# A fused attention block whose matrix work is all put into 64x32 tiles, in one order per step

## The reference, cut to what matters

```python
x = x + attn(layernorm(x))
x = x + ffn(layernorm(x))          # ternary weights, 4-bit and 8-bit activations, inner size 1376

q, k, v = proj(w_q), proj(w_k), proj(w_v)        # (2, 32, 1024, 16)
scores = einsum('bhqd,bhkd->bhqk', q, k) / sqrt(16)
out = einsum('bhqk,bhkd->bhqd', softmax(scores), v)
attn = einsum('bse,oe->bso', out, w_o)
```

## Time and profile before

| | |
|---|---|
| time, median of 3 runs (lowest to highest) | 963.26 us (963.06 to 964.16) |
| profiled execution: its time, its span | 963.78 us, 962.0 us |
| mean granted clock of TensorE | 0.987 |
| busy share of the span: PE, PEld, DVE, ACT, POOL | 93%, 31%, 88%, 78%, 24% |
| the same from 200 to 700 us | 96%, 27%, 95%, 87%, 31% |
| score, transposed score, projection piece, values: mean duration of one matmul | 384, 385, 377, 606 ns |
| DVE maximum, ACT exponential: mean duration of one | 683, 606 ns |

### The profile page before, as it was taken

One profiled execution on the slowest core, in us unless ns is written; L12 is line 12 of the kernel. 1 busy time (PEld: TensorE's weight loads), 2 busy tenths in 40 slices (PEclk: granted clock), 3 DMA queues, 4 the chain that ended last, 5 costly groups with the idle time before them and its releaser, 6 DMA issues.

```text
span 962.0 us, 17694 instructions
## 1 busy us (share of the span) xinstructions
PE 894.6 (93%) x6232; PEld 294.7 (31%) x6232; DVE 847.1 (88%) x1576; ACT 750.3 (78%) x1468; POOL 233.8 (24%) x367
## 2 busy tenths in 40 slices
PE   4799999999999999999999999999999998999986
PEld 3333222222222222222222222222222224454442
DVE  6877799999999999999999999999999667788975
ACT  4422499888888898899888888888888976777784
POOL 3600011162111111821363431421043222000000
PEclk9989899999999999999999999999999998999999
DMA  8340021121114122331413223141231202111000
GB/s 308 88 161 2 1 54 42 40 56 41 40 34 125 51 88 56 97 100 34 107 45 87 60 81 85 27 113 48 78 122 35 57 20 73 65 46 45 22 34 33
DMA packets 40573, 64.96 MB, mean 68 GB/s; under 512 B 5926, under 2 KB 20774, under 8 KB 40486
## 3 DMA queue, kind: packets, MB, share of 16 engines
q1 hardware_dynamic: 40486, 63.85, 23.2%
HBM read 42.27 MB, written 21.23 MB: 66 GB/s over the span
## 4 chain that ended last, share of the span: by engine, by line
PE 46%; DVE 31%; ACT 10%; issue 6%; DMA 3%; SPq 2%; POOL 1%; ACTq 0%; DVEq 0%; POOLq 0%
DVE mx L1008 22%; PE ps L490 16%; PE ps L410 12%; PE ps L469 8%; ACT PB L775 5%; PE ps L326 5%; DVE XV L1105 2%; PE ps L606 2%; PE ps L635 1%; PE ps L570 1%; ACT XV L845 1%; DMA tu<-wkT 1%; DVE hm L1114 1%; ACT XV L840 1%; ACT PB L856 1%
## 5 line engine op out<-in xcount | busy, mean ns | idle before, releaser
L1008 DVE TENSOR_REDUCE mx<-ps 128x1 f32<-128x512 f32 x1024 | 636.6, 683 | 44.4 <-PE ps L410 42.3
L775 ACT ACTIVATE PB<-ps 128x512 f32<-128x512 f32 x1024 | 537.4, 606 | 77.5 <-PE ps L469 76.3
L410 PE MATMUL ps<-QK 48*128 48x512 f16 x1024 | 334.9, 384 | 27.9 <-DVE mx L1008 23.5
L469 PE MATMUL ps<-QK 50*128 50x512 f16 x1024 | 314.1, 385 | 4.0 <-ACT PB L775 1.4
L490 PE MATMUL ps<-PB,Vg 128*32 128x512 f32 x2048 | 273.3, 606 | 0.0
L410 PEld LDWEIGHTS ps<-QK 48*128 48x128 f16 x1024 | 89.2, 94 | 309.2 <-DVE mx L1008 232.0
L388 PE MATMUL ps<-XV,wqk 64*128 64x512 f16 x624 | 160.6, 377 | 0.0
L469 PEld LDWEIGHTS ps<-QK 50*128 50x128 f16 x1024 | 76.4, 94 | 109.0 <-ACT PB L775 84.8
L1272 POOL TENSOR_SCALAR nmb<-nm 128x16 f16<-128x16 f32 x32 | 6.5, 203 | 366.8 <-DVE nm L1013 366.5
L845 ACT ACTIVATE XV<-XV,magic,hm 128x512 f32<-128x512 f32 (+1 forms) x48 | 33.5, 760 | 40.0 <-DVE hm L1130 40.0
L490 PEld LDWEIGHTS ps<-PB,Vg 128*32 128x32 f32 x2048 | 40.7, 108 | 66.2 <-issue 44.8
(11 more groups left out here) (164 smaller groups left out, 787.2 us busy)
## 6 DMA issues: line engine op xcount, KB each, us to landing
parts_d<-spl SPq DMA_DIRECT2D x64, 128.0 KB
att_d<-OS SPq DMA_DIRECT2D x32, 256.0 KB
XV<-x SPq DMA_DIRECT2D x28, 256.0 KB, 5.3
QK<-parts_d SPq DMA_DIRECT2D x48, 128.0 KB, 2.6
QK<-parts_d SPq DMA_DIRECT2D x16, 256.0 KB, 4.2
XV<-att_d SPq DMA_DIRECT2D x8, 512.0 KB, 3.4
XV<-rden_d SPq DMA_DIRECT2D x8, 512.0 KB, 4.7
out<-PB SPq DMA_DIRECT2D x16, 256.0 KB, 2.0
```

The source lines that it names most:

```text
L410: nc.tensor.matmul(ps[:, at % S_BANKS, :], QK[rows, sup % 2, 2 * set_ + p, 0, half * HALF + qt * P:half * HALF + (qt + 1) * P], QK[rows, s ...
L469: nc.tensor.matmul(ps[:, T_BANK + t_slot(n) % T_BANKS, :], QK[rows, sup % 2, 2 * set_ + p, 1, kt * P:(kt + 1) * P], QK[rows, sup % 2, 2 * ...
L775: nc.scalar.activation(PB[:, at % 3, 2 * (i // 2) + t_side(step, i), :], ps[:, T_BANK + t_slot(n) % T_BANKS, :], ACT.Exp, scale=exp_reg).t ...
L1008: nc.vector.tensor_reduce(mx[:, v % 2, idx, kh:kh + 1], ps[:, at % S_BANKS, :], AX.X, ALU.max).then_inc(s_used, 1)
```

## The change

All matrix work of a step, except in units 30 and 31, is issued for tiles of 64 rows by 32 columns of the array.

- A score, a transposed score and a projection piece are each cut into four strips of 32 stationary columns (`STRIPS`), with the same moving operand and the same bank. One instruction pair (load, multiply) becomes four. The semaphore is counted by the last strip.
- The values of a step are cut into two halves of 64 keys (side 0, side 1), and each half into two parts of 256 queries. The parts are put between the other pieces of the step. At the first key tile side 0 is issued whole. Side 1 waits for side 0 (`av_half`), and side 0 of the next step for side 1 of this one (`av_done`), since both add to one bank.
- All steps of units 0 to 29 have one order. The sides are fixed: scores 1, 1, 0, 0; transposed scores 1, 0, 0, 1; pieces 1, 1, 0, 0. Pieces of one job are taken in another order, and the wait between sides (`job_turn`) comes every two pieces.
- Scores issued before the first superunit, and the transposed scores and values of units 30 and 31, stay as they were (`strips=1`, `side=None`). The pieces that fall in unit 30 (one step) are in strips too.

```diff
@@ -42,6 +42,9 @@
 AUG = ROWS + 2
 AUX_HIGH, AUX_LOW = 32768.0, 8.0
 HALF_RANGE = 32768.0
+STRIP = 32
+STRIPS = P // STRIP
+JOB_PIECES = 6 * KT
 EXPONENT = 0x7F800000
 IT = (INTER + P - 1) // P
 ILAST = INTER - (IT - 1) * P
@@ -70,8 +73,8 @@
 WCOL = KT * INTER
 DCOL = IT * HID
 ROW_SLOT = 20
-SIDES = (0, 1, 1, 0)
-SCORE_SIDES = ((0, 0, 0, 0), (1, 0, 0, 1), (1, 0, 0, 1), (1, 1, 1, 1), (0, 0, 0, 0), (1, 1, 1, 1), (0, 0, 0, 0), (1, 1, 1, 1))
+SIDES = (1, 0, 0, 1)
+SCORE_SIDES = (1, 1, 0, 0)
 
 
 def build(nc, x, wqT, wkT, wvT, woT, wgT, wuT, wdT, s_gate, s_up, s_down, out):
@@ -228,6 +231,7 @@
         rows_psum, rows_used = sem("rows_psum"), sem("rows_used")
         nm_in = [sem(f"nm_in{r}") for r in range(2)]
         st_psum, probs, av_done = sem("st_psum"), sem("probs"), sem("av_done")
+        av_half = sem("av_half")
         os_copy, os_out = sem("os_copy"), [sem(f"os_out{r}") for r in range(2)]
         wo_whole = sem("wo_whole")
         wo_sum, wo_step, wo_scale, wo_parts, o_back = (sem("wo_sum"), sem("wo_step"), sem("wo_scale"), sem("wo_parts"),
@@ -273,8 +277,8 @@
 
             if v < EARLY_UNITS:
                 return k // 8, k // 4 % 2, k % 2, k // 2 % 2
-            side = SCORE_SIDES[k // 4][k % 4]
-            c = sum(SCORE_SIDES[i // 4][i % 4] == side for i in range(k))
+            side = SCORE_SIDES[k % 4]
+            c = 2 * (k // 4) + k % 2
             return c // 4, c // 2 % 2, side, c % 2
 
         def av_bank(unit):
@@ -361,18 +365,19 @@
             if m == 3 * KT - 1:
                 last.then_inc(job_psum, 1)
 
-        def pe_job_half(pe, n, side, m):
-
+        def pe_job_half(pe, n, piece):
+
+            side, m = 1 - piece // 2 % 2, piece // 4 * 2 + piece % 2
             k, (a, b) = m // 3, PRODUCTS[m % 3]
-            first_piece, last_piece = (side, m) == (0, 0), (side, m) == (1, 3 * KT - 1)
+            first_piece, last_piece = piece == 0, piece == JOB_PIECES - 1
             if first_piece:
                 if n > JOBS_AHEAD:
                     pe.wait_ge(os_copy, n - JOBS_AHEAD)
                 else:
                     pe.wait_ge(rows_used, 1)
                 pe.wait_ge(w_low, 5)
-            elif m % 4 == 0:
-                pe.wait_ge(job_turn, 5 * (n - JOBS_AHEAD) + 2 * (m // 4) + side)
+            elif piece % 2 == 0:
+                pe.wait_ge(job_turn, (JOB_PIECES // 2 - 1) * (n - JOBS_AHEAD) + piece // 2)
             rows = slice(side * SIDE, side * SIDE + SIDE)
             if n < JOBS:
                 sup, qk, half = job_of(n)
@@ -385,13 +390,15 @@
                     pe.wait_ge(att_parts, SPB)
                     pe.wait_ge(wo_parts, 1)
                 stationary, moving = attp[0][rows, a, k, t * P:(t + 1) * P], wop[rows, b, k, :]
-            last = nc.tensor.matmul(ps[:, job_bank(n), :], stationary, moving, start=first_piece, stop=last_piece)
+            for c in range(STRIPS):
+                strip = slice(c * STRIP, c * STRIP + STRIP)
+                last = nc.tensor.matmul(ps[strip, job_bank(n), :], stationary[:, strip], moving, start=first_piece, stop=last_piece)
             if last_piece:
                 last.then_inc(job_psum, 1)
-            elif m % 4 == 3:
+            elif piece % 2:
                 last.then_inc(job_turn, 1)
 
-        def pe_scores(pe, sup, unit, k):
+        def pe_scores(pe, sup, unit, k, strips):
 
             qt, p, side, kh = item_of(sup * 4 + unit, k)
             set_, half = unit // 2, unit % 2
@@ -407,13 +414,13 @@
             else:
                 pe.wait_ge(s_used, at - S_BANKS + 1)
             rows = slice(side * SIDE, side * SIDE + ROWS)
-            nc.tensor.matmul(ps[:, at % S_BANKS, :],
-                             QK[rows, sup % 2, 2 * set_ + p, 0, half * HALF + qt * P:half * HALF + (qt + 1) * P],
-                             QK[rows, sup % 2, 2 * set_ + p, 1, kh * HALF:(kh + 1) * HALF],
-                             start=True, stop=True).then_inc(s_psum, 1)
-
-        def t_side(step, i):
-            return SIDES[i] if step % KEYT in (1, 2, 3, 5, 7) else 1 - SIDES[i]
+            width = P // strips
+            for c in range(0, P, width):
+                last = nc.tensor.matmul(ps[c:c + width, at % S_BANKS, :],
+                                        QK[rows, sup % 2, 2 * set_ + p, 0, half * HALF + qt * P + c:half * HALF + qt * P + c + width],
+                                        QK[rows, sup % 2, 2 * set_ + p, 1, kh * HALF:(kh + 1) * HALF],
+                                        start=True, stop=True)
+            last.then_inc(s_psum, 1)
 
         def t_slot(n):
 
@@ -453,11 +460,11 @@
                                            nmb[:, qt, :, :, :].rearrange("p s a h -> p (s a h)"), identh[:])
             last.then_inc(rows_psum, 1)
 
-        def pe_scoresT(pe, sup, step, i):
+        def pe_scoresT(pe, sup, step, i, strips):
 
             unit, kt = step // KEYT, step % KEYT
             set_, half = unit // 2, unit % 2
-            side, p = t_side(step, i), i // 2
+            side, p = SIDES[i], i // 2
             n = sup * 4 * STEPS + 4 * step + i
             if kt == 0 and i == 0:
                 pe.wait_ge(nm_in[half], sup * 64 + 32 * (set_ + 2))
@@ -466,18 +473,21 @@
                     pe.wait_ge(v_copy, TILES)
             t_slot_wait(pe, t_slot(n))
             rows = slice(side * SIDE, side * SIDE + AUG)
-            nc.tensor.matmul(ps[:, T_BANK + t_slot(n) % T_BANKS, :],
-                             QK[rows, sup % 2, 2 * set_ + p, 1, kt * P:(kt + 1) * P],
-                             QK[rows, sup % 2, 2 * set_ + p, 0, half * HALF:(half + 1) * HALF],
-                             start=True, stop=True).then_inc(st_psum, 1)
-
-        def pe_av(pe, sup, step):
+            width = P // strips
+            for c in range(0, P, width):
+                last = nc.tensor.matmul(ps[c:c + width, T_BANK + t_slot(n) % T_BANKS, :],
+                                        QK[rows, sup % 2, 2 * set_ + p, 1, kt * P + c:kt * P + c + width],
+                                        QK[rows, sup % 2, 2 * set_ + p, 0, half * HALF:(half + 1) * HALF],
+                                        start=True, stop=True)
+            last.then_inc(st_psum, 1)
+
+        def pe_av(pe, sup, step, side, part=0):
 
 
             unit, kt = step // KEYT, step % KEYT
             set_, at = unit // 2, sup * 4 + unit
             pe.wait_ge(probs, sup * 4 * STEPS + (4 * step + 4))
-            if kt == 0:
+            if kt == 0 and side != 1 and part == 0:
                 if unit % 2 == 0:
                     pe.wait_ge(vg_ready, sup * 2 + (set_ + 1))
                 if job_in(at - 1):
@@ -486,70 +496,86 @@
                     pe.wait_ge(os_copy, at - 1)
                 if at == 1:
                     pe.wait_ge(rows_used, 1)
+            if side is None:
+                for h in range(GH):
+                    last = nc.tensor.matmul(ps[32 * h:32 * h + 32, av_bank(at), :], Vg[:, set_, kt, h, :],
+                                            PB[:, (sup * STEPS + step) % 3, h, :], start=(kt == 0), stop=(kt == KEYT - 1))
+                last.then_inc(av_done, 1)
+                return
+            n = sup * STEPS + step
+            if side and part == 0:
+                pe.wait_ge(av_half, n + 1)
+            elif n > 0 and part == 0:
+                pe.wait_ge(av_done, n)
+            rows = slice(side * SIDE, side * SIDE + SIDE)
+            whole = kt == 0 and side == 0
+            if whole and part:
+                return
+            queries = slice(0, HALF) if whole else slice(part * HALF // 2, (part + 1) * HALF // 2)
             for h in range(GH):
-                last = nc.tensor.matmul(ps[32 * h:32 * h + 32, av_bank(at), :], Vg[:, set_, kt, h, :],
-                                        PB[:, (sup * STEPS + step) % 3, h, :], start=(kt == 0), stop=(kt == KEYT - 1))
-            last.then_inc(av_done, 1)
+                last = nc.tensor.matmul(ps[32 * h:32 * h + 32, av_bank(at), queries], Vg[rows, set_, kt, h, :],
+                                        PB[rows, n % 3, h, queries], start=whole,
+                                        stop=(kt == KEYT - 1 and side == 1 and part == 1))
+            if part or whole:
+                last.then_inc(av_done if side else av_half, 1)
 
         def pe_superunit(pe, sup, last):
 
             def item(step, j):
                 ahead, unit, k = step_items(step)[j]
                 if not (last and ahead):
-                    pe_scores(pe, sup + ahead, unit, k)
+                    pe_scores(pe, sup + ahead, unit, k, STRIPS)
+            def lagging(step, side, part=0):
+                if step > 1:
+                    pe_av(pe, sup, step - 2, side, part)
+                elif sup > 0:
+                    pe_av(pe, sup - 1, STEPS - 2 + step, side, part)
+
             for step in range(STEPS):
                 at, r = sup * 4 + step // KEYT, step % KEYT
```

(48 more changed lines are left out.)

## The result

The changed kernel takes 1014.55 us (median of 4 runs, 1007.57 to 1015.24) against 963.16 us before: ratio 1.052, 95% interval 1.050 to 1.054. It is slower by 51 us where 27 us less were forecast. The profiled execution took 1014.58 us, its span 1012.8 us.

A forecast was written before the change was run, and what follows sets the result against it. It saw a ring of waits, not a single bound engine, with DVE setting the pace afterwards. Plain units 18.2 + ABS units 5.4 + reciprocal units 4.2 - 0.4 = 27.4 us saved from 963.8: 936 us, range 922 to 966.

The forecast's parts named there:

- DVE as the floor: Attention stage: after the change DVE sets the pace, 32 x 0.597 + 0.21 = 19.3 us a unit.
- A quartet takes a slot: Strips on PE: four run side by side and take the slot of one matmul, 0.216 us.
- the 0.24 us at the ends of the block: PE streams nothing for 0.10 us ahead of and 0.14 behind each step's values; both were to go.
- New waits: Semaphores between the four parts of the values: 0.25 us to spare in a DVE step of 2.39, so costed at nothing.
- chain of halves: The halves of a step's values following each other through semaphores: 0.86 us and a 0.21 handover each, 2.14 a step.
- The 0.25 us to spare: Slack claimed for the 2.14 us chain of the values' halves within a DVE step of 2.39 us.
- The sign that the prediction named for this: Trace sign of a wrong forecast: the values' weight load waits for the values before, pointing to the halves' chain.
- their fetch is not priced here: PE's instructions grow about threefold over the stage; their fetch got no cost and was left to the issue rival.
- slower by pairs: Rival: from 0.031 us a pair PE issues too slowly; at 0.056, about 1,400 us; chance 0.11.
- slower by the chain of halves: Rival: DVE-blocked scores delay the next half; 2.54 us a step at 0.1 each, 985 us at 0.15; chance 0.08.
- Reciprocal units: Units where DVE waits 2.4 us for denominators from memory: about 0.45 of the gain lost there, 0.6 x 7 = 4.2 saved.
- The sum: Savings of plain, ABS and reciprocal units less 0.4 us: 27.4 us from 963.8, giving 936 us.

The follow-up runs named there:

- e4: The changed kernel without the wait on the exponentials (`probs`) ahead of the parts of the values, so one wait a link: 948.79 us, ratio 0.985.
- e12: e4 with scores, transposed scores and pieces as one whole 64x128 tile each, values in 64x32 between them: 2176.31 us, ratio 2.26.
- e13: e4 with `av_half` counted one slot later, by the third strip of the next transposed score, with no second wait: 972.63 us, ratio 1.009.
- e11: e4 with DVE's reciprocal of the denominators in the last step of its unit instead of the last but one: 942.83 us, ratio 0.978.
- e14: The changed kernel with the double wait on `av_half` only, the link by `av_done` having one wait: 972.83 us, ratio 1.006.
- e6: e4 with a long satisfied second wait ahead of the second and third transposed score of each step, off the chain: 959.02 us, ratio 0.995.
- e10: e4 with an old `av_done` waited for ahead of `s_used` in two scores a step, off the chain: 958.85 us, ratio 0.995.
- e9: The changed kernel with its two waits exchanged, `av_half` or `av_done` first and `probs` second: 968.54 us, ratio 1.002.

## Why the prediction was wrong, by its steps

- *DVE as the floor, 19.3 us a unit*: right. e4 reaches 19.3 to 19.4 where no pause falls into a unit.
- *A quartet takes a slot; the 0.24 us at the ends of the block go*: right. In e12, without strips, the values don't run beside the other pieces.
- *New waits, costed at nothing.* This is the step that failed. "A step's chain of halves is 2 x (0.86 + 0.21) = 2.14 us" took the handover from TensorE to DVE, 0.21, for the one from TensorE to itself. It measured 0.37 with a double wait (2.48 a step) and about 0.30 with a single one (2.31). The 0.25 us to spare were not there. The sign that the prediction named for this, the values' weight load waiting for the values before, stood mostly under "issue" in the trace. By e13, a chain of 2.50 us a step costs 24 us; the changed kernel's own length then comes to about 19 us, an estimate in proportion to what lies above 2.39.
- *"their fetch is not priced here"*: the other part, a term put at nothing. Fetches of 256 instructions were never closer than 3.3 us, the step of 160 instructions leaves each 3.9 to 4.0, and the changed kernel loses 60 us at the boundaries where e4 loses 16. The rival "slower by pairs" named the number of pairs, but as a rate at every pair; the cost came in pauses of up to 4 us. With the 19 us of the chain and the 13 us of the last point here, these 44 us make 76 of the 79 us by which the forecast was too low.
- *Rival "slower by the chain of halves"*: its place was right, its size too (2.48 a step against the 2.54 assumed), its mechanism not: blocked scores were not needed, the handover was.
- *Reciprocal units*: the mechanism was right. DVE's waits for memory rose from 2.4 to 5.4 us in e4, and e11 gives 6 us back.
- *The sum*: with one wait a link, 948.8 us, against 936 predicted: 13 us short. The boundary time rose by about as much (16 us against 2), and the half clock holds for 20 us between 200 and 700 us, where it did not before; how the two share the 13 us is not shown.

What stays open: why a double wait costs so much more at a boundary when it stands on the chain (e14, two such: 60 us) than when it stands off it, satisfied or not (e6, e10: 29 and 26 us). Length of the chain is not it (e13), order within the pair is most of it (e9). The table above shows that the next fetch starts later, by 0.9 us with two double waits on the chain and by some 0.1 us or less off it. Why a standing wait on the chain delays the fetch, and one off it (e10) hardly does, no run shows. That TensorE's instructions behind a standing wait are not taken in is argued. Open too is what the pauses would be without the transfers of the other queues.

The Trainium skill ("TensorE: Matmul & The Clock Gate", "Wait — 56ns, not 53.3ns?") offered 62 ns a matmul where microcode decodes. 80 pairs in a step of 2.39 us (e4) are 30 ns, so the traces exclude it here.

## What to carry to other kernels

If matmuls are cut into more and smaller instructions, count the instructions as well as the array time: here the fetches of 256 of TensorE's were never closer than 3.3 us, and a step that used 256 in 3.9 us lost time to them, the more where large transfers ran beside them. Give an instruction on a tight chain one wait only; where two are needed, write first the one that really waits, and drop those that an earlier wait of the same engine implies: dropping them alone turned 1.052 into 0.985. Take the price of a handover from the same pair of engines, not from the nearest other one.

## What the runs showed of the hardware that was not expected

- A matmul with two waits carries the first on its weight load; the second is an instruction of its own, and it costs 0.08 us where it waits on the chain (link 546 ns against 464).
- Pauses of TensorE of 1 to 4 us stand at one place in each 256 of its instructions (15 of 17 in the changed kernel), the longest where the program has no wait, and they end 1.2 to 2.0 us after a fetch of 16,384 bytes has landed. Such fetches were never closer than 3.3 us in any kernel.
- In e4 all six boundary pauses over 1 us came where other transfers kept 0.89 or more of the DMA engines' time, ahead of the fetch.
- Two double waits a step on a tight chain moved the start of the next fetch from 0.96 us (e4) to 1.89 us after the last place (changed kernel).
- With shapes of 64x128 and 64x32 in turn, the granted clock stayed at 0.50 from 200 to 700 us with PE counted busy for all 500 us.
